# Three layer normalisations moved from VectorE to ScalarE, a rounding from ScalarE to GpSimd, and a new written order for five engines

## The reference

```
# block 0: two layers; hidden h, adj as it is
u = h @ h^T / sqrt(D);  a = softmax(u);  delta = a * adj
attn = delta / (sum(delta) + 1e-10)
ctx = (attn*upper) @ (h@Wl^T + bl) + diag(attn) * (h@Ws^T + bs) + (attn*lower) @ (h@Wr^T + br)
h = relu(layernorm(ctx, 1e-12) * g + beta)
x = layernorm(x + h)
# block 1: 12 heads of 32
scores = q @ k^T / sqrt(32) + beta * adj, masked to -9e15 where adj is 0
x = layernorm(x + softmax(scores) @ v)
```

## Time and profile before

| | |
|---|---|
| median of 3 runs | 1998.94 us (1995.54 to 2000.99) |
| the profiled execution, its own time | 2005.07 us |
| its span | 2003.3 us |
| PE, DVE, ACT, POOL busy | 1762.5, 1643.9, 1184.8, 808.9 us |
| mean granted clock of PE | 0.962 |

### The profile page before, as it was taken

One profiled execution on the slowest core, in us unless ns is written; L12 is line 12 of the kernel. 1 busy time (PEld: TensorE's weight loads), 2 busy tenths in 40 slices (PEclk: granted clock), 3 DMA queues, 4 the chain that ended last, 5 costly groups with the idle time before them and its releaser, 6 DMA issues.

```text
span 2003.3 us, 39999 instructions
## 1 busy us (share of the span) xinstructions
PE 1762.5 (88%) x13120; PEld 1658.7 (83%) x13120; DVE 1643.9 (82%) x5479; ACT 1184.8 (59%) x2844; POOL 808.9 (40%) x780
## 2 busy tenths in 40 slices
PE   5799889989998999999899899999989999998962
PEld 4798888889887888888888888888888888898852
DVE  4578888978887988888888788888888898888865
ACT  3366656656665665666566566666656665665543
POOL 1333433444443434354344344434434443544331
PEclk9899999999999999999999999999999999999975
DMA  4046656556556565565655665656555656556464
GB/s 145 27 103 134 131 106 133 128 122 140 129 127 119 128 138 119 131 136 116 123 132 127 126 131 119 130 120 140 128 123 118 134 124 133 127 135 133 101 126 102
DMA packets 550037, 247.66 MB, mean 124 GB/s; under 512 B 423100, under 2 KB 549832, under 8 KB 549832
## 3 DMA queue, kind: packets, MB, share of 16 engines
q1 hardware_dynamic: 538928, 231.91, 54.1%
q10 hardware_dynamic: 10904, 13.20, 2.3%
...
## 4 chain that ended last, share of the span: by engine, by line
PE 51%; DVE 30%; DMA 10%; issue 5%; ACT 2%; SPq 1%; POOL 1%; ACTq 0%; POOLq 0%; DVEq 0%
PE bank_w L382 26%; DMA pT<-halves 9%; PE bank_m L382 9%; PE bank_u L382 6%; DVE halves L871 6%; DVE prob L866 4%; PE bank_s L382 3%; PE bank_o L382 3%; DVE hT_bl L741 2%; DVE qk_lo L845 2%; DVE hlrl L771 2%; DVE normed L810 2%; DVE y_in L839 1%; PE bank_t L399 1%; DVE stats_y L827 1%
## 5 line engine op out<-in xcount | busy, mean ns | idle before, releaser
L664 ACT ACTIVATE prob<-prob,hmin 128x256 f32<-128x256 f32 x768 | 345.8, 500 | 27.3 <-DVE hmin L866 25.1
L672 ACT ACTIVATE halves<-prob 128x512 f16<-128x512 f32 x384 | 240.3, 626 | 184.1 <-DMA pT<-halves 183.3
L871 DVE TENSOR_TENSOR halves<-prob,halves 128x512 f16<-128x512 f32 x384 | 279.7, 728 | 50.2 <-ACT halves L672 48.8
L866 DVE CUSTOM_DVE_ANT_0 prob<-bank_s,bias_adj 128x256 f32<-128x256 f32 x768 | 292.8, 419 | 22.7 <-PE bank_s L382 12.9
L958 POOL TENSOR_SCALAR v_rest<-adj_in 128x512 f32<-128x512 f32 x32 | 65.9, 2061 | 405.8 <-issue 405.8
L382 PE MATMUL bank_o<-v_parts,pT 128*128 128x99 bf16 (+1 forms) x3072 | 183.8, 208 | 37.0 <-DMA pT<-halves 28.8
L382 PE MATMUL bank_w<-w_graph0h,hT_ach 128*128 128x384 f32 x576 | 207.7, 361 | 7.3 <-DVE w_graph0l L724 5.7
L382 PE MATMUL bank_w<-hT_ach,w_qkvh 128*128 128x256 f32 x576 | 175.2, 304 | 36.4 <-DVE qk_lo L845 35.4
L382 PEld LDWEIGHTS bank_o<-v_parts,pT 128*128 128x128 f16 x3072 | 138.1, 101 | 82.1 <-DMA pT<-halves 40.1
L382 PE MATMUL bank_s<-k_st,q_st 96*128 96x256 f32 x768 | 160.3, 304 | 49.1 <-issue 35.6
L382 PE MATMUL bank_w<-w_graph1h,hT_bh 128*128 128x384 f32 x576 | 197.6, 343 | 0.0
...
## 6 DMA issues: line engine op xcount, KB each, us to landing
...
q_st<-qk_hi SPq DMA_DIRECT2D x256, 96.0 KB, 2.3
k_st<-qk_hi SPq DMA_DIRECT2D x256, 96.0 KB, 2.8
q_st<-qk_lo SPq DMA_DIRECT2D x128, 96.0 KB, 2.2
k_st<-qk_lo SPq DMA_DIRECT2D x128, 96.0 KB, 2.4
...
pT<-halves SPq DMA_TRANSPOSE x384, 3.1
```

The lines of the kernel that those rows point to most:

```text
L664: nc.scalar.activation(prob[:, k % 2, i, :], prob[:, k % 2, i, :], ACT.Exp, bias=hmin[:, i, k:k + 1], scale=-1.0).then_inc(s_prob, 1)
L672: nc.scalar.activation(halves[:, k % 2, :, 0, :], prob[:, k % 2, :, :], ACT.Copy).then_inc(s_pt_hi, 1)
L866: ve.tensor_tensor_reduce(prob[:, k % 2, i, :], bank_s[k % 2][:, i * S:(i + 1) * S], bias_adj[:, i, :], -SCALE, BIG, ALU.add, ALU.min, hmi ...
L871: ve.tensor_tensor(halves[:, k % 2, :, 1, :], prob[:, k % 2, :, :], halves[:, k % 2, :, 0, :], ALU.subtract).then_inc(s_pt_lo, 1)
```

## The change

Three of the four applications move to ACT: DVE now makes only a 128x2 shift (-mean * rstd, `shifted`) after the refinement, and ACT computes scale * x + shift over 128x384, twice for each norm. The fp16 rounding of the probabilities moves from ACT to POOL with the same waits. The lists in ORDER are new for all five engines.

```
--- before.py
+++ after.py
@@ the table
     "pool": """
-        a_turn.0-1 q.0 c_sum.0 v.0 q.2 b_turn.0 v.1 b_apply.0""",
+        weights.7-1 a_turn.0-1 weights.8-1 weights.9-1 weights.10-1 weights.11-1 q.0 c_sum.0 q.2 weights.0
+        weights.1 v.0 b_turn.0 weights.2 v.1 weights.3 weights.4 weights.5 b_apply.0 weights.6""",
@@ ACT
+            def scaled(dst, src, k, index, done):
+                act.wait_ge(s_shift[k], index + 1)
+                for i in range(NT):
+                    nc.scalar.activation(dst[:, i, :], src[:, i, :], ACT.Identity, bias=shift[k][:, i:i + 1],
+                                         scale=rstd[k][:, i:i + 1]).then_inc(done, 1)
+            def h_apply(t, _k):
+                scaled(normed, mixed, "a", t - 1, s_h1)
+            def b_out(t, _k):
+                if t != 1:
+                    act.wait_ge(s_res, t - 1)
+                scaled(y_in, normed, "y", t - 1, s_y)
+            def c_apply(t, _k):
+                scaled(result, result, "c", t - 3, s_out_ok)
-            def weights(t, k):
-                s = t - 2
-                act.wait_ge(s_prob, NT * (NH * s + k + 1))
-                wait(act, s_pt[k % 2], 16 * (NH // 2 * s + k // 2))
-                nc.scalar.activation(halves[:, k % 2, :, 0, :], prob[:, k % 2, :, :], ACT.Copy).then_inc(s_pt_hi, 1)
@@ DVE
+            def shifted(k):
+                settle()
+                ve.scalar_tensor_tensor(shift[k][:, :], mv[k][:, :, 0], -1.0, rstd[k][:, :], ALU.mult, ALU.mult
+                                        ).then_inc(s_shift[k], 1)
             def h_apply(t, _k):
                 refine("a", t - 1, inv_s["a"][:, :])
-                for i in range(NT):
-                    ve.tensor_scalar(normed[:, i, :], mixed[:, i, :], mv["a"][:, i, 0:1], rstd["a"][:, i:i + 1],
-                                     ALU.subtract, ALU.mult).then_inc(s_h1, 1)
+                shifted("a")
...
@@ POOL
+            def weights(t, k):
+                s = t - 2
+                pool.wait_ge(s_prob, NT * (NH * s + k + 1))
+                wait(pool, s_pt[k % 2], 16 * (NH // 2 * s + k // 2))
+                gp.tensor_copy(halves[:, k % 2, :, 0, :], prob[:, k % 2, :, :]).then_inc(s_pt_hi, 1)
```

More of the change, by code:

```diff
@@ L47 @@
     "pe": """
-        scores.10-1 turn_y.1-1 a_mix.0-1 attend.6-1 attend.7-1 turn_y.2-1 a_mix.1-1 q.0 scores.11-1 q.1 q.2
-        attend.8-1 k.0 attend.9-1 turn_h.0 k.1 k.2 turn_h.1 v.0 attend.10-1 turn_h.2 v.1 attend.11-1 turn_x.0
-        b_scores.0 turn_x.1 scores.0 b_proj.0 scores.1 b_proj.1 b_proj.2 turn_x.2 scores.2 b_proj.3 b_turn.0
-        b_proj.4 b_proj.5 scores.3 scores.4 a_scores.0 b_mix.0 attend.0 scores.5 scores.6 b_mix.1 attend.1
-        a_proj.0 a_proj.1 scores.7 a_turn.0 a_proj.2 attend.2 attend.3 a_proj.3 a_proj.4 scores.8 attend.4
@@ L61 @@
[L61 to L68 removed]
+        scores.10-1 turn_y.1-1 a_mix.0-1 turn_y.2-1 attend.6-1 a_mix.1-1 q.0 attend.7-1 q.1 q.2 scores.11-1
```

66 lines of the change are left out of this document (32 added, 34 removed).

## The result

The changed kernel is slower: 2061.82 us (median of 4 runs, 2051.29 to 2065.45) against 1997.24 us on the same chip, ratio 1.0315 with a 95% interval of [1.0269, 1.0362]. The forecast was 1927, and 1985 at most. The profiled execution took 2051.29 us, its span is 2049.5 us, the mean granted clock 0.951.

The account below looks back on a forecast made before the run. About half the round was taken to hang on PE's own work, half on DVE chains PE waits for. Terms -0.9 - 1.3 - 0.8 + 0.6 = -2.4 us, times about 30 rounds, gave 1927 us; range 1872 to 1985.

Parts of the forecast that it names:

- stretch 1: Part of a round from the end of b_mix.1 on PE to PE's first turn of y; forecast -0.9 us.
- The 0.73 us of the longer way through ACT: Norm y: shift, reaching ACT and two ACT passes take 1.60 us against 0.87 on DVE, 0.73 longer.
- The 1.99 us of steps that no longer stand ahead: On DVE ahead of norm y: scores.5 (0.76 us), scores.8 (0.76) and a_proj.4 (0.47) are moved behind.
- Collisions: DVE and POOL instructions meeting: a one-input cast on POOL costs DVE about 0.1 us a meeting.
- The rival of full exclusion: Each cast makes a two-input DVE instruction wait to its end: 1.3 us a round, 1966 us; chance 0.12.
- Stretches 2 and 3: From PE's first turn of y to its first turn of h, -1.3 us; then to the second, -0.8 us.
- Stretch 4: From PE's second turn of h to the end of b_mix.1: two attends arrive from elsewhere, +0.6 us.
- The cast: POOL's rounding of 128x512 from f32 to fp16, taken as 0.69 us each, 12 casts a round.
- DVE down by 80 us: Sign of being right: DVE's busy time falls by 80 us in all over the kernel.
- POOL's queue: Rival: casts waiting for transposes at POOL's head delay b_apply and a_turn, +2.5 us a round, 2074 us; chance 0.13.
- The 0.5 us a round: Cost put for late POOL steps and collisions, with the same 0.5 taken back from the long rounds.
- long rounds: About each third round, near 62 us against 58, where DMAs come in; rival that they vanish: 1882 us, chance 0.15.

Follow-up runs that it names:

- weights.6 alone: The changed kernel with only DVE's weights.6 moved one place later, behind norm y's shift (b_out): 1994.52 us, ratio 0.9974.
- the kernel with the norms alone: The kernel before with the three norms on ACT, rounding still on ACT, old lists with the new ACT steps put in: 2071.96 us, ratio 1.0363.

## Why the prediction was wrong

**The failing step** is the way through stretch 1: "14.29 - 1.99 + 0.73 = 13.0 us ... PE sets it. Stretch 1: -0.9 us". On the mean it went from 15.38 to 17.32, +1.9 us. By the table of norm y above, the two terms came out like this.

- The 0.73 us of the longer way through ACT was right, but it was only part of the way. From the start of the refinement to the first turn of y it is 1.50 us before and 3.94 after, 2.44 more. Of that 1.7 us is the holding of the four small instructions by POOL, and 0.7 the longer way.
- The 1.99 us of steps that no longer stand ahead brought the refinement forward by 0.44 us only. DVE has 1.6 us less to do in front of it, but waits 1.16 us more: 1.64 us a round for POOL's casts (0.78 at head 4, 0.85 at head 6), where it had waited 0.53 for ACT's roundings.

The step weights.6 ties the two together. Its own 0.6 us stood ahead of y before too (ahead of the aggregation), so the sum owed nothing for that. What it lacked was a price for an item that now waits on POOL, which waits on a transpose, directly ahead of four small instructions that POOL's next work holds. Moving this one step gave back 67 us where 65 had been lost: that is shown. The split is worked out from means.

That PE's own work sets the stretch was wrong as well. PE is busy 13.7 us of it, near the forecast's 13.4, and waits 3.5 us besides: 2.1 for y and 1.4 ahead of a_proj.2. The second wait had no term in the forecast, and in no run did it shrink without another wait or hold growing in its place. With weights.6 alone stretch 1 is 15.4 us, 2.0 us a round above the 13.4 forecast, and the time is 67 us above the forecast 1927. So what made the change slower than before is shown, and why it is not faster is shown only in part.

**Collisions** failed in the size: "a cast, with one input, costs DVE about 0.1 us a meeting". Measured alone it is 0.36 us, and on norm y's chain of four small instructions, each of which can meet another POOL instruction, 1.7 us a round. The row that the 0.1 us was read from was a TENSOR_SCALAR's, not a cast's. The rival of full exclusion had the mechanism, but spread it evenly over the round (1.3 us, still faster than before); it is the concentration on one chain that PE waits for that made it dear.

**Stretches 2 and 3.** Forecast -1.3 and -0.8, measured -0.7 and -0.7. The second is right, and by its reason (hT_bl 878 to 420 ns). The first has the right mechanism: in the 12 of 27 rounds at full clock stretch 2 is 11.4 to 11.5 us as forecast (11.3), and in the other 15, at 0.75 to 0.87, it is 13.1 on the mean. That this is only PE's wait for y is not shown: with weights.6 alone that wait is 0.20 us and the clock 0.96, and the stretch is still 12.5 us, with 0.23 us a round of PE waiting for POOL's triangles, which had not been there. **Stretch 4**: +0.6 forecast, +0.9 measured. **The cast**: 0.69 forecast, 0.654 measured.

**DVE down by 80 us**: it went down by 4.2. The passes left it, but its small instructions and others were held for most of that time. In the kernel with the norms alone it went down by 71 us, and the time rose. The busy time saved was not what the round hung on.

**The rival that came out nearest in time**, POOL's queue (2074 us), was right that casts at the head of POOL would be late and wrong about who pays, so that its time (2074) lies near the measured 2062 by luck: in the changed kernel no PE row shows a wait for the triangles. DVE paid, at weights.4 and weights.6, where "DVE waiting for the cast at weights.4 to 7" had been listed as a sign of error. **The 0.5 us a round** put against the long rounds was a guess on both sides; the long rounds did not go away, rounds of 62 to 64 us still occur.
